# New orders at the head and the tail of a one-core attention and mixture-of-experts kernel, with cheaper routing and norm steps

## The reference

```python
# first half: x -> x1
h = layernorm(x)
latent = h @ W_basis.T                         # 64 wide
v = h @ W_v.T + b_v
att = softmax(causal(latent @ latent.T / 8))   # per batch
x1 = x + layernorm((att @ v) @ W_o.T + b_o)
# second half: x1 -> out
h = layernorm(x1)
scores = sigmoid(h @ gate_w.T)                 # 64 experts
choice = scores + gate_bias
group_score = sum of the two largest of choice in each of 8 groups
masked = choice in the 4 best groups, 0 elsewhere
picked = the 8 largest of masked
rw = 2.5 * scores[picked] / (sum(scores[picked]) + 1e-20)
routed = sum over experts e of rw[e] * (silu(h @ Wg[e].T) * (h @ Wu[e].T)) @ Wd[e].T
out = x1 + layernorm(routed + shared_mlp(h))
```

## Time and profile before

| | |
|---|---|
| median of 3 runs | 477.61 us (476.32 to 477.9) |
| the profiled execution's own time | 477.6 us |
| its span | 475.6 us |
| PE busy | 455.8 us (96%) |
| POOL, DVE, ACT busy | 335.9, 325.5, 286.0 us |
| mean granted TensorE clock | 0.983 |

### The profile page before, as it was taken

The page is one execution under the profiler, slowest core; times in us unless marked ns, Lnnn a source line. Parts: engine busy times, 40 slices in busy tenths (PEclk is TensorE's granted clock), DMA queues, the critical chain, the costliest instruction groups (busy, mean ns, idle before and its releaser), DMA issues.

```text
span 475.6 us, 8043 instructions
## 1 busy us (share of the span) xinstructions
PE 455.8 (96%) x2152; PEld 370.5 (78%) x2152; DVE 325.5 (68%) x694; ACT 286.0 (60%) x573; POOL 335.9 (71%) x318
## 2 busy tenths in 40 slices
PE   6999986999999999999999999999999999999995
PEld 4889774767778888888888888888888888888894
DVE  5666989786466666666666666666666666666786
ACT  2577985855665565565556555555655555566563
POOL 6853667765677767777776777777677777768674
PEclk8899997999999999999999999999999999999999
DMA  7000000000010100001010000101000010100002
GB/s 180 25 3 2 18 17 19 17 1 0 1 51 19 34 17 20 31 17 33 17 33 17 23 26 17 33 17 33 17 22 28 17 33 17 33 0 0 0 23 67
DMA packets 12856, 11.58 MB, mean 24 GB/s; under 512 B 2549, under 2 KB 12837, under 8 KB 12837
## 3 DMA queue, kind: packets, MB, share of 16 engines
q1 hardware_dynamic: 11973, 11.02, 8.0%
q10 hardware_dynamic: 864, 0.33, 0.4%
HBM read 10.30 MB, written 1.05 MB: 24 GB/s over the span
## 4 chain that ended last, share of the span: by engine, by line
PE 89%; ACT 5%; DVE 2%; issue 2%; DMA 1%; ACTq 0%; POOL 0%; DVEq 0%
PE ps L1303 27%; PE ps L1305 26%; PE ps L1304 26%; PE ps L1255 2%; PE ps L1243 1%; PE ps L1203 1%; PE ps L1274 1%; PE ps L1298 1%; PE ps L1195 1%; PE ps L1223 1%; PE ps L1224 1%; PE ps L1454 1%; DMA bv_sb<-in_b_v 1%; ACT xn L672 1%; ACT exp_t L712 1%
## 5 line engine op out<-in xcount | busy, mean ns | idle before, releaser
L547 POOL TENSOR_TENSOR lat_hi<-hid,lat_hl 128x512 fp32r<-128x512 f32 (+1 forms) x187 | 239.9, 1285 | 101.5 <-ACT lat_hl L768 97.1
L754 ACT ACTIVATE ps<-ps 128x512 f32<-128x512 f32 (+1 forms) x180 | 103.1, 573 | 132.1 <-PE ps L1305 131.8
L1005 DVE TENSOR_TENSOR up_w<-ps,route_w 128x512 f32<-128x512 f32 (+1 forms) x180 | 122.2, 679 | 85.2 <-PE ps L1305 84.7
L1015 DVE TENSOR_TENSOR hid<-ps,up_w 128x512 f32<-128x512 f32 (+1 forms) x180 | 122.4, 680 | 33.6 <-DVE up_w L1005 28.3
L1303 PE MATMUL ps<-x_hi,w_hi 128*128 128x512 f32 (+1 forms) x360 | 141.2, 392 | 2.8 <-ACT route_w L740 2.4
L1305 PE MATMUL ps<-x_hi,w_lo 128*128 128x512 f32 (+1 forms) x360 | 140.5, 390 | 0.0
L1304 PE MATMUL ps<-x_lo,w_hi 128*128 128x512 f32 (+1 forms) x360 | 140.2, 389 | 0.0
L768 ACT CAST lat_hl<-hid 128x512 fp32r<-128x512 f32 (+1 forms) x188 | 113.4, 605 | 14.2 <-DVE hid L1015 11.7
L1303 PEld LDWEIGHTS ps<-x_hi,w_hi 128*128 128x128 f32 x360 | 68.0, 189 | 19.4 <-issue 4.3
L1305 PEld LDWEIGHTS ps<-x_hi,w_lo 128*128 128x128 f32 x360 | 68.1, 189 | 15.0
L1304 PEld LDWEIGHTS ps<-x_lo,w_hi 128*128 128x128 f32 x360 | 68.0, 189 | 14.5
(11 more groups left out here) (140 smaller groups left out, 366.9 us busy)
## 6 DMA issues: line engine op xcount, KB each, us to landing
w_raw<-in_w_experts SPq DMA_DIRECT2D x44, 192.0 KB, 2.4
x_sb<-in_x SPq DMA_DIRECT2D x3, 256.0 KB, 4.9
out<-x_sb SPq DMA_DIRECT2D x3, 256.0 KB, 2.3
x_sb<-in_x ACTq DMA_DIRECT2D x2, 64.0 KB, 2.3
x_sb<-in_x SPq DMA_DIRECT2D x2, 64.0 KB, 2.1
out<-x_sb SPq DMA_DIRECT2D x1, 128.0 KB, 1.8
out<-x_sb SPq DMA_DIRECT2D x2, 64.0 KB, 1.6
sh_raw<-in_w_shared_up SPq DMA_DIRECT2D x1, 88.0 KB
```

The costliest lines, as they stand in the source:

```text
L547: g.tensor_tensor(hid_lo[:, k % DEEP, 0:w], hid[:, k % 2, 0:w], hid_hi[:, k % DEEP, 0:w], ALU.subtract).then_inc(s_hlo, 1)
L754: a.activation(bank, bank, ACT.Silu).then_inc(s_gated, 1)
L1005: v.tensor_tensor(up_w[:, k % 2, 0:w], ps[:, gate_bank(k) + 1, 0:w], route_w[:, group, 512 * q + lo:512 * q + lo + w], ALU.mult).then_inc( ...
L1015: v.tensor_tensor(hid[:, k % 2, 0:w], ps[:, gate_bank(k), 0:w], up_w[:, k % 2, 0:w], ALU.mult).then_inc(s_hid, 1)
```

## The change

1. All eight order tables are written anew. The steady loop is as it was.
2. Quad 0's rstd comes from a square root on ACT and a reciprocal on DVE; POOL's two operations for it go. ACT loads the square root's table behind its first two loads of x, ahead of the issues of the weights, and the exponential's table after the square root. xn of quad 0 is handed to PE tile by tile. Eight warm-up matmuls instead of ten, and one more after P0.
3. The scaled high part of the latent is made from lat_hi in SBUF, after it; DVE waits for lat_hi alone, PE for both.
4. x1's mean is x's own (the attention branch is already centred), negated by POOL at stage S. DVE's statistics of x1 go; ACT sums the squares instead (square_x1, stage X in ACT_ORDER), and POOL makes power and shift of them.
5. The mask of the groups is one DVE scalar_tensor_tensor; the comparison on DVE and the product on POOL go. masked has two buffers. 1e-20 stands in a 65th column of left and 2.5 in the selection matrix, so one DVE operation per quad goes.
6. The tail: the last chunk's down product runs with centred weights (made at stage C of the tail) and adds straight to the turned result, 2 x 3 matmuls of 128 columns; the last two units take their variance from squares on ACT and a square root. 
7. Most new buffers stand behind the others; masked, left, wc, wc_hi and group_in shift those between.

```diff
         PE_ORDER = stages(
-            "P0 Q0 K0 V0 A00 P1 A01 A02 Q1 T00 T02 A03 C00 C01 T04 T06 A10 C02 C03 A11 P2 V1 "
+            "P0 Q0 K0 A00 V0 A01 A02 P1 Q1 T00 A03 T02 C00 T04 C01 T06 A10 C02 C03 A11 T10 P2 "
...
         POOL_ORDER = stages(
-            "S0 S1 P1 B0 S2 P2 D0 S3 P3 X0 D1 F0 X1 L0 J0 D2 E0 R0 M0 F1 R1 X2 E1 L1 J1 D3 E2 "
-            "F2 M1 W0 R2 J2 W1 X3 R3 W2 W3 W4 M2 F3 W5 W6 E3 W7 W8 J3 W9 W10 W11 W12 M3 W13 "
+            "S1 P1 S2 P2 D0 S3 P3 B0 L0 X0 D1 E0 F0 X1 R0 D2 M0 F1 R1 L1 E1 X2 D3 R2 F2 X3 W0 "
+            "R3 W1 E2 M1 W2 W3 W4 M2 W5 F3 W6 W7 W8 W9 W10 W11 M3 W12 W13 W14 E3 W15 W16 W17 "
...
+            def inv_sqrt_x1(q):
...
+                link(g.tensor_scalar(var_e[:], x1_var[:, q], 1.0 / C, EPS, ALU.mult, ALU.add))
+                link(g.tensor_tensor(rstd[:, k], var_e[:], minus_half[:], ALU.pow))
+                pool.wait_ge(s_mean, q + 1)
+                g.tensor_tensor(shift[:, k], neg_mean[:, q], rstd[:, k],
+                                ALU.mult).then_inc(s_rstd, 1)
...
-            def mask_groups(q):
...
-                a.copy(lat_hi[:, own], ps[:, 1, :])
-                a.activation(lat_hl[0:R, own], ps[0:R, 1, :], ACT.Identity,
-                             scale=SCALE).then_inc(s_lhi, 1)
+                a.copy(lat_hi[:, own], ps[:, 1, :]).then_inc(s_lhi, 1)
+                act.wait_ge(s_lhi, q + 1)
+                a.activation(lat_hl[0:R, own], lat_hi[0:R, own], ACT.Identity,
+                             scale=SCALE).then_inc(s_lhs, 1)
...
+            def square_x1(q):
+
+                act.wait_ge(s_x1, q + 1)
+                act.wait_ge(s_mean, q + 1)
+                for t in range(4):
+                    ins = a.activation(x1_squares[:, t], x1_sb[:, 4 * q + t, :], ACT.Square,
+                                       bias=neg_mean[:, q, t:t + 1],
+                                       accum_out=x1_var[:, q, t:t + 1])
+                ins.then_inc(s_x1var, 1)
...
+            act.wait_ge(s_eps, 1)
+            a.activation(first_dev[:, 4:5], eps_col[:], ACT.Sqrt)
             a.dma_start(wv_sb[:], w_v).then_inc(s_wvl, 16)
...
+            act.wait_ge(s_var, 1)
+            a.activation(first_dev[:, 0:4], mv[:, 0, :, 1], ACT.Sqrt,
+                         bias=eps_col[:]).then_inc(s_dev0, 1)
+            a.activation(first_dev[:, 5:6], eps_col[:], ACT.Exp)
...
+            def norm_x0():
+                dve.wait_ge(s_dev0, 1)
+                v.reciprocal(rstd[:, 0], first_dev[:, 0:4]).then_inc(s_rstd, 1)
+                dve.wait_ge(s_rstd, 1)
...
-                tt(group_in[:], group_left[:], group_score[:], ALU.not_equal).then_inc(s_gin, 1)
+                v.scalar_tensor_tensor(
+                    out=masked[:, q % 2].rearrange("p t (g k) -> p t g k", k=GE),
+                    in0=group_left[:, :, :].unsqueeze(3).to_broadcast([P, 4, GROUPS, GE]),
+                    scalar=TAKEN, in1=choice[:, q % 2].rearrange("p t (g k) -> p t g k", k=GE),
+                    op0=ALU.is_equal, op1=ALU.mult).then_inc(s_masked, 1)
...
-                link(v.tensor_scalar(wsum[:], wsum[:], 1e-20, 1.0 / ROUTED_SCALE, ALU.add,
-                                     ALU.mult))
...
+            def last_down(k):
+
+                pe.wait_ge(s_wclo, 1)
+                pe.wait_ge(s_hlast, 1)
+                for t in range(2):
+                    own = slice(P * t, P * t + P)
+                    to = ps[:, unit_bank(len(UNITS) - 1), own]
+                    hi, lo = hid_hi[:, k % DEEP, own], hid_lo[:, k % DEEP, own]
+                    t_.matmul(to, hi, wc_hi[:], start=False, stop=False, skip_group_check=True)
+                    t_.matmul(to, hi, wc_lo[:], start=False, stop=False, skip_group_check=True)
+                    mm = t_.matmul(to, lo, wc_hi[:], start=False, stop=True,
+                                   skip_group_check=True)
+                mm.then_inc(s_yp, 1)
```

More of the change, by code:

```diff
@@ L613, in _ @@
                     add_bias(q)
-                elif what == "J":
-                    mask_groups(q)
                 elif what == "L":
@@ L791, in _ @@
                     keep_att(q, n // 2)
+                elif what == "X":
+                    square_x1(q)
                 elif what == "Y":
@@ L835, in _ @@
                     act.wait_ge(s_eps, 1)
-                    a.activation(deviation[:, 2:3], eps_col[:], ACT.Sqrt)
+                    a.activation(deviation[:, 0, 2:3], eps_col[:], ACT.Sqrt)
                 elif what == "Y":
-                    act.wait_ge(s_var, len(VARIANCES) + k + 1)
-                    a.activation(deviation[:, 0:2], mv[:, 2 + k % 2, 0:2, 1], ACT.Sqrt,
+                    act.wait_ge(s_yp, k + 1)
+                    for t in range(UNITS[k][2]):
+                        ins = a.activation(squares[:, t, 0:C], ps[:, unit_bank(k), P * t:P * t + P],
+                                           ACT.Square, scale=float(C) ** -0.5,
+                                           accum_out=y_var[:, k % 2, t:t + 1])
+                    ins.then_inc(s_yvar, 1)
+                    act.wait_ge(s_yvar, k - len(UNITS) + 3)
+                    a.activation(deviation[:, k % 2, 0:2], y_var[:, k % 2], ACT.Sqrt,
                                  bias=eps_col[:]).then_inc(s_dev, 1)
+                elif what == "C":
+                    act.wait_ge(s_wc, 1)
+                    a.copy(wc_hi[:], wc[:]).then_inc(s_wchi, 1)
                 elif what == "O":
@@ L1037, in _ @@
                     add_attention(q)
-                elif what == "X":
-                    dve.wait_ge(s_x1, q + 1)
-                    if q >= 2:
-                        dve.wait_ge(s_xn2, q - 1)
-                    statistics(2 + q % 2, lambda t: x1_sb[:, 4 * q + t, :])
                 elif what == "G":
@@ L1093, in _ @@
                     hidden(k, LAST_S + k, w)
+                elif what == "C":
+                    dve.wait_ge(s_wl[SETS - 1], 16 * ROUNDS)
+                    rows = w_raw[:, SETS - 1, WD:WD + P]
+                    link(v.bn_stats(wc_stats[:], rows))
+                    link(v.bn_aggr(wc_mean[:], wc_stats[:]))
+                    v.tensor_scalar(wc[:], rows, wc_mean[:, 0:1], None,
+                                    ALU.subtract).then_inc(s_wc, 1)
                 elif what == "O":
-                    dve.wait_ge(s_down, LAST_S + unit_step(k) + 1)
+                    dve.wait_ge(s_down, LAST_S + unit_step(k))
                     dve.wait_ge(s_yt, k)
@@ L1375, in _, with keep_busy @@
             pe.wait_ge(s_const, 1)
-            for _ in range(10):
-                t_.matmul(ps[:, 6, 0:P], ident[:], ident[:], start=True, stop=True)
+            def keep_busy(n):
+                for _ in range(n):
+                    t_.matmul(ps[:, 6, 0:P], ident[:], ident[:], start=True, stop=True)
+            keep_busy(8)
             for at, (what, q, n) in enumerate(PE_ORDER):
@@ L1443, in _ @@
                         down(kd, LAST_S + kd, q, w_hi[:, c, :], w_lo[:, c, :], P,
-                             start=(lo > 0 and c == 0), stop=(c == SETS - 1), lo=lo, w=w)
+                             start=(lo > 0 and c == 0),
+                             stop=(c == SETS - (2 if lo else 1)), lo=lo, w=w)
                 elif what == "T":
```

167 lines of the change are left out of this document (93 added, 74 removed), and 35 rows, old and new, of tables (ACT_ORDER, DVE_ORDER, PE_ORDER, POOL_ORDER).

## The result

The change makes the kernel slightly slower: the median of 11 runs went from 476.32 us (475.61 to 477.90) to 478.60 us (478.04 to 479.48), a ratio of 1.0043 with a 95% interval of 1.0031 to 1.0055. The forecast was 471.7 us, with a range of 466.5 to 475.8. It was wrong, and in its sign too.

The account below looks back on a forecast made before the run. PE was taken to bound the kernel, fully busy from 160 to 430 us. Head -2.5, ACT +0.6, stall -3.1, 84 to 160 0, end -0.9 sum to -5.9: 477.6 to 471.7 us, range 466.5 to 475.8.

Parts of the forecast that it names:

- head, quad 0 and POOL: Head, to about 16 us: first copy and second latent come earlier, -2.5 us, bounds -4.0 and -1.5.
- in the stall: The mask had no term of its own; its savings were counted in the long stall's -3.1 us.
- The addresses: Moving w_hi and w_lo by 896 bytes was costed at nothing; 1 ns a loop matmul would make +1.3 us.
- The sign that I named for it: Loop: a mean other than 0.231 us a matmul would show the forecast wrong.
- The squares: ACT, 24 to 70: squares cost 1.1 us a quad, half of net +1.2 on PE's path: +0.6, bounds 0 and +2.2.
- The chain x1, squares, power, Y is no longer than through DVE: Head, second half's input: the route through ACT's squares was claimed no longer than the old one through DVE.
- ACT becomes the bound: Rival, 43 to 73: unhidden squares and late copies leave PE idle; +2.8 in all, 480.4 us, chance 0.06.
- The head's start: Quad 0: transposes done at 6.3 us and the first xn_t copy ended at 6.9 to 7.0 instead of 8.98.
- second latent at 13.9: Head, quad 1: DVE's statistics end at 7.4, so the second latent comes at 13.9 instead of 16.56, 2.6 us earlier.
- The low clock that I counted as won between 8 and 16: Head: PE kept at work, so the latent takes 1.07 us at full clock instead of 1.89 at the low one.
- The stall and 84 to 160: Stall, 70 to 85: shorter waits, no low clock, G1's weights at 79.4, -3.1 us; 84 to 160: 0, bounds -1.5 and +1.5.
- The end: Tail: a shorter chain against one table load, last multiply at 471.8 instead of 472.75, -0.9 us, bounds -1.6 and +0.4.

Follow-up runs that it names:

- b_tail: The kernel before with part 6 and the four tail order tables of the change, no old buffer moved: 475.47 us, ratio 0.9979.
- b_tail_sq: b_tail plus part 2 (square root on ACT and reciprocal for quad 0), other head orders as before: 474.03 us, 0.9946 of the kernel before.
- b_tail_mask: b_tail plus part 5 (mask of the groups in one DVE operation), orders of before: 474.84 us, 0.9971 of the kernel before.
- b_all_lhs: b_all plus part 3 (scaled high part made from lat_hi in SBUF): 473.39 us, 0.9933 of the kernel before.
- b_all: The change without part 3, the squares on ACT and the new head orders, at the addresses of before: 473.53 us, 0.9934 of the kernel before.
- b_all_x: b_all with the squares of x1 on ACT in place of DVE's statistics: 477.37 us, 1.0017 of the kernel before.
- a_addr: The change with route_w, the shared weights, w_raw, w_hi and w_lo back at their addresses of before: 475.58 us, 0.9985 of the kernel before.
- a_oldorder: a_addr with the four head order tables of before, adapted to the changed parts: 477.67 us, 1.0035 of the kernel before.
- a_dvex: The change with the statistics of x1 back on DVE and no squares on ACT, its own orders otherwise: 479.78 us, 1.0082 of the kernel before.
- b_shiftw: The kernel before with 896 empty bytes ahead of w_hi, so that only w_hi and w_lo move: 478.73 us, ratio 1.0068.

## Why the prediction was wrong

By ratios to the kernel before, and 476.3 us:

| step | forecast | measured | from |
|---|---|---|---|
| tail | -0.9 | -1.0 | b_tail |
| head, quad 0 and POOL | -2.5 | -1.6 | b_tail_sq less b_tail |
| mask | in the stall | -0.4 | b_tail_mask less b_tail |
| scaled part from SBUF | 0 | 0 | b_all_lhs less b_all |
| squares on ACT, old orders | +0.6 | +4.0 | b_all_x less b_all |
| new head orders, all parts | -3.1 | -2.4 | a_addr less a_oldorder |
| addresses | 0 | +2.8 | the change less a_addr |

The rows add up to +1.4, and the change measured +2.0. The step between the fifth and the sixth row is missing: a_oldorder is 0.0018, or 0.9 us, above b_all_x, and differs from it by part 3 alone. The intervals do not part that from nothing. Each row carries an uncertainty of 0.7 to 1.6 us.

**The addresses were the step that turned the sign.** I wrote "I cost at nothing: no row shows a matmul that differs by the chunk it reads". That was true of the rows and proved nothing, as the chunks of one buffer lie 1536 bytes apart, a multiple of 512, and so all have one place modulo 512. I even had the size right ("1 ns in the loop's 1296 matmuls, it would be +1.3"; it was 1.8 ns and 2.4 us), and then left it out of the sum and out of the range. The sign that I named for it, a mean other than 0.231 us, is what gave it away.

**The squares were mis-sized in two places.** The price, "4 x 0.278, or 1.1 us a quad, priced by the like operation on 129 columns", left out that operation's read of the accumulator and took an operation without a bias from SBUF for one with it: 0.391 and 0.189 us, which overlap to 1.55 us for the quad. The row of the change decides, and the Trainium skill (ScalarE: Activation LUTs, What ACT_TABLE_LOAD costs) would have given the first of the two: 280 + 0.833 x 128 is an estimated 387 ns with a bias pointer. "Of which I put half on PE's path" was the second: in the old orders 4.0 of the four quads' 6.2 us counted. "The chain x1, squares, power, Y is no longer than through DVE" failed in the old orders too: it begins when ACT's queue gets to it, 7.4 us after x1 of quad 0 was ready in b_all_x, and POOL's 1.6 us hang behind. In the change itself it did not fail at quad 0, for there ACT waited for x1 (the row at 35.57). So the 4.0 us are a price in the old orders; what the squares cost within the new ones no run isolates, and a_dvex shows only that DVE's statistics, put into the same orders, cost more.

The rival "ACT becomes the bound" had 3.8 us for this, from 43 to 73, and said it decides from a PE wait of over 3 us. PE's idle time there rose by 0.8 us (4.15 to 4.93). It rose more from 36 to 48, where PE fell from 11.83 to 9.96 us of 12, in five waits of 0.2 to 0.9 us and at a granted clock of 1.00. I had given the rival 0.06.

**The new DVE_ORDER held x1 back**, which the prediction did not price at all: x1 of quad 0 was ready 5.5 us later than before. Of the first product's delay below, 2.0 us are the new orders by themselves (67.15 in a_addr against 65.20 in a_oldorder).

**The head's start** came 1.0 us late: the eight warm-up matmuls filled PE from 2.78 for 3.78 us by the modelled ends, P0 came behind them at 6.36, and the copy ended at 8.04, not 7.0. The POOL half of that step (second latent at 13.9) failed on the load of x. And "that is the median of the runs too" held for three runs, not for eleven. The low clock that I counted as won between 8 and 16 is not in all executions of the kernel before. Here is b_shiftw, whose head is that of before, instruction for instruction:

```profile
8.00:16.00 8.00, 5.38 (x31) 3.78 (x29) 5.11 (x23) 3.05 (x7) 6.70 (x9) 1.00 0.56 155
...
131.81 0.69 DVE L1016 TENSOR_TENSOR hid<-ps,up_w 128x512 f32<-128x512 f32 x1 [0.99 <-ACT ps L755]
```

Its loop begins at 131.81, 1.7 us earlier than in the execution that I forecast from, and 2.05 earlier than in the changed kernel. Of the 1.7, 1.33 are there when x1 of quad 0 begins (27.39 against 28.72).

**The stall and 84 to 160** were about right as a difference, but in another way. The first product of the second half came 3.9 us late (67.9 against 64.0), the sixth 1.0 late (87.4 against 86.4), so the new order won 2.9 of the 3.1, and a further 0.7 until the loop began, 0.33 late. But PE did not get by without the low clock: it ran at 0.57 from 72 to 76, after the waits around 71.6, and G1 stood at 83.6, not at 79.4.

**The end** was right: -0.96 with the addresses restored (44.53 us from the loop's last product to the end of the span, against 45.49). Both table loads were followed at once by the next operation, at 6.03 and 471.62, so the doubled switch, by which the estimate was 474.1, did not occur.

## What to carry to other kernels

When a change moves a buffer that the inner loop reads, restore its address with a pad and time both, before anything else is concluded; and where the sum puts a term at nothing only because no row can show it, keep its size in the range. An operation that moves to the bounding engine can cost most of its time (here 4.0 of 6.2 us), and whatever of its chain runs on other engines can only start when that queue reaches it. After reordering, look first at when the value that the second half waits for is ready (here x1). Judge a set of parts by adding them one at a time to the old orders: here three parts were worth 3 us, and one took back 4.
